# Mixer A of a hybrid layer: the turns of one shared PSUM bank moved to other steps of a selective scan

## What is computed

```python
xn = rmsnorm(layernorm(x)) * norm_w
x_part, z = split(xn @ in_proj_w.T)
u = silu(causal_conv(x_part, conv_w, 4 taps) + conv_b)
dt, B, C = split(u @ x_proj_w.T)              # 8, 16 and 16 columns
delta = softplus(dt @ dt_proj_w.T + dt_proj_b)
h = exp(delta * A) * h + delta * B * u        # for each time step, 256 x 16 states
y = (h * C).sum(states) + u * D
out = (y * silu(z)) @ out_proj_w.T + residual
```

## The kernel before

| use | writer on PE | reader |
|---|---|---|
| TAPS0, TAPS1 | convolution, 4 taps, two at a step (L334) | ACT, bias added, into u (L488) |
| PROJECT (chunk g - 1) | output projection (L364) | DVE `add` (L582), end of step 4 |
| XPROJ | dt, B and C rows (L352) | ACT `keep_rows` (L464, L465), then DVE `low_rows` (L570), end of step 7 |
| DT0, DT1 | dt projection (L358) | ACT `parts` (L468, L469) |
| Z0, Z1 | gate input z (L340) | ACT copy (L516) |

## Time and profile before

### The profile page before, as it was taken

The page is one execution under the profiler, slowest core; times in us unless marked ns, Lnnn a source line. Parts: engine busy times, 40 slices in busy tenths (PEclk is TensorE's granted clock), DMA queues, the critical chain, the costliest instruction groups (busy, mean ns, idle before and its releaser), DMA issues. The chain is left out here.

```text
span 1163.9 us, 16413 instructions
## 1 busy us (share of the span) xinstructions
PE 1014.3 (87%) x4830; PEld 718.0 (62%) x4830; DVE 750.9 (65%) x1167; ACT 609.5 (52%) x1154; POOL 575.7 (49%) x455
## 2 busy tenths in 40 slices
PE   5887879788788889999999787896897899999997
PEld 2222323232246669999998444653575689999996
DVE  4788777779929755555555476755469555555555
ACT  5665453555335345555554486667542455555553
POOL 2368565567710488733851364631000887454732
PEclk9889889789978999999999888997978999999999
DMA  4122111212231113321110400000320223111103
GB/s 134 57 60 67 47 63 46 64 53 71 59 121 55 56 33 93 77 83 60 35 42 15 111 1 1 1 1 0 103 73 3 70 82 91 52 53 59 53 26 113
DMA packets 57248, 66.41 MB, mean 57 GB/s; under 512 B 6088, under 2 KB 40656, under 8 KB 57168
## 3 DMA queue, kind: packets, MB, share of 16 engines
q1 hardware_dynamic: 52176, 55.13, 15.3%
q0 software_dynamic: 4992, 10.23, 3.6%
HBM read 54.86 MB, written 10.49 MB: 56 GB/s over the span
## 5 line engine op out<-in xcount | busy, mean ns | idle before, releaser
L687 POOL TENSOR_TENSOR a_hc<-a_h,a_c_sb 128x512 f32<-128x512 f32 x128 | 160.4, 1267 | 105.1 <-DVE a_h L608 90.2
L533 ACT ACTIVATE ps<-a_delta,a_neg_a 128x512 f32<-128x512 f32 x128 | 87.7, 688 | 125.9 <-DVE a_h L608 125.4
L419 PE MATMUL ps<-a_hc,eye 128*128 128x512 f32 x256 | 141.4, 669 | 12.1 <-POOL a_hc L687 11.9
L419 PEld LDWEIGHTS ps<-a_hc,eye 128*128 128x128 f32 x256 | 49.3, 211 | 85.6 <-issue 50.9
L592 DVE TENSOR_TENSOR a_b_u<-a_du,ps 128x1024 f32<-128x1024 f32 x64 | 76.6, 1196 | 38.5 <-PE ps L406 38.4
L879 POOL CAST g_ring_rounded<-g_ring 128x1876 fp32r<-128x1876 f32 x8 | 14.1, 1761 | 153.1 <-DVE g_table L1394 103.5
L608 DVE TENSOR_TENSOR_SCAN a_h<-ps,a_state,a_b_u 128x512 f32<-128x512 f32 x64 | 78.8, 1262 | 0.0
L1023 PE MATMUL ps<-g_ring_rounded,g_q_hi_rounded 128*128 x312 | 77.0, 337 | 0.0
L1023 PE MATMUL ps<-f_ring_rounded,f_q_hi_rounded 128*128 x312 | 77.0, 337 | 0.0
L608 DVE TENSOR_TENSOR_SCAN a_h<-ps,a_b_u 128x512 f32<-128x512 f32 x64 | 75.1, 1206 | 0.2
L879 POOL CAST f_ring_rounded<-f_ring 128x1876 fp32r<-128x1876 f32 x8 | 14.1, 1759 | 115.0 <-DVE f_table L1394 70.7
(11 more groups left out here) (450 smaller groups left out, 2874.0 us busy)
## 6 DMA issues: line engine op xcount, KB each, us to landing
a_c_sb<-c_rows SPq DMA_DIRECT2D x64, 256.0 KB, 3.2
f_ring<-in_gu SPq DMA_DIRECT2D x16, 469.0 KB, 4.6
g_ring<-in_gu SPq DMA_DIRECT2D x16, 469.0 KB, 4.4
f_ring<-in_dn SPq DMA_DIRECT2D x8, 512.0 KB, 6.2
g_ring<-in_dn SPq DMA_DIRECT2D x8, 512.0 KB, 5.7
xn_rows<-f_work SPq DMA_DIRECT2D x8, 256.0 KB, 2.6
f_rows<-token_rows SPq DMA_DIRECT2D x8, 256.0 KB, 4.9
xn_rows<-g_work SPq DMA_DIRECT2D x8, 256.0 KB, 2.6
```

The costliest lines, as they stand in the source:

```text
L419: nc.tensor.matmul(ps[:, Y + f, :], k.eye[:, :], hc[:, s % WAITING, :], start=False, stop=(n == NST - 1)).then_inc(y_added, 1)
L533: nc.scalar.activation(ps[:, A + m % NA, :], delta[:, f, cols(g)], ACT.Exp, scale=neg_a[:, f, n:n + 1])\
L687: nc.gpsimd.tensor_tensor(hc[:, m % WAITING, :], h[:, s % DEPTH, :], c_sb[:, i % RING, :], ALU.mult)\
```

## The change

Only numbers in four `between` parts change. In step or half-step numbers, with the chunk that is being scanned:

| use | PE step | reader's half-step on ACT |
|---|---|---|
| TAPS0, both tap pairs | 0, 1 (as before) | 4 -> 2 |
| TAPS1, both tap pairs | 2, 3 -> 3, 4 | 8 -> 7 |
| PROJECT | 4 -> 6 | (DVE, end of step 4, as before) |
| XPROJ | 6 -> 8 | 14 -> 15 (DVE, end of step 7, as before) |
| DT0, DT1 | 8, 9 -> 10, 12 | 18, 20 -> 19, 23 |
| softplus exp, log | | 21, 22 -> 24, 25 |
| Z0, Z1 | 11, 12 -> 14, 15 | 25, 27 -> 27, 30 |

On POOL delta goes from half-step 21 to 24, du from 23 to 26, and the addition to x from 27 to 14. The queues of DVE and SP hold the same instructions in the same order. No instruction is added or taken away, and each keeps its waits.

```diff
@@ PE
-                    if n in (0, 2):
-                        in_turn(g, TAPS0 + n // 2)
-                    if n in (1, 3):
-                        convolution(g + 1, n // 2, O, TAPS // 2, TAPS).then_inc(o_ready, 1)
-                if g and n == 4:
+                    if n in (0, 3):
+                        in_turn(g, TAPS0 + n // 3)
+                    if n in (1, 4):
+                        convolution(g + 1, n // 4, O, TAPS // 2, TAPS).then_inc(o_ready, 1)
+                if g and n == 6:
                     in_turn(g, PROJECT)
...
@@ POOL
-                    if s == 27:
+                    if s == 14:
                         pool.wait_ge(norm.normed, g + 1)
```

More of the change, by code:

```diff
@@ L385, in between @@
                 if g + 1 < NCH:
-                    if n in (0, 2):
-                        in_turn(g, TAPS0 + n // 2)
-                    if n in (1, 3):
-                        convolution(g + 1, n // 2, O, TAPS // 2, TAPS).then_inc(o_ready, 1)
-                if g and n == 4:
+                    if n in (0, 3):
[3 more added lines that the diff above has]
+                if g and n == 6:
                     in_turn(g, PROJECT)
                 if g + 1 < NCH:
-                    if n == 6:
+                    if n == 8:
                         in_turn(g, XPROJ)
[L395 to L398, removed]
+                    if n in (10, 12):
+                        in_turn(g, DT0 + (n - 10) // 2)
+                    if n in (14, 15):
+                        in_turn(g, Z0 + n - 14)
             def broadcast(m):
@@ L484, in between @@
                 if c < NCH:
-                    if s in (4, 8):
-                        f = s // 8
+                    if s in (2, 7):
+                        f = s // 7
                         turn(g, TAPS0 + f)
@@ L500, in between @@
                 if c < NCH:
-                    if s == 14:
+                    if s == 15:
                         turn(g, XPROJ)
                         keep_rows(c, O)
-                    if s in (18, 20):
-                        f = (s - 18) // 2
+                    if s in (19, 23):
+                        f = (s - 19) // 4
                         turn(g, DT0 + f)
                         parts(c, f, O).then_inc(o_read, 1)
-                    if s == 21:
+                    if s == 24:
                         softplus_exp(c)
-                    if s == 22:
+                    if s == 25:
                         softplus_log(c)
                         nc.scalar.preload_act_table_set("exp_and_others")
-                    if s in (25, 27):
-                        f = (s - 25) // 2
+                    if s in (27, 30):
+                        f = (s - 27) // 3
                         turn(g, Z0 + f)
@@ L694, in half_sequence @@
                                 .then_inc(delta_ready, 1)
-                        if s == 23:
+                        if s == 26:
                             pool.wait_ge(delta_ready, g + 2)
```

## The result

The changed kernel takes 1121.08 us (median of four runs, 1114.49 to 1122.36) against 1169.82 before (a fourth run, 1170.82, has joined the three of the table); the ratio is 0.958, with a 95% interval of 0.954 to 0.962. The profiled execution, at 1114.49 the fastest of them, has a span of 1112.7 us, 51.2 less than before. The last `add` of mixer A now ends at 281.70 us in place of 328.45, and the scan started at the same time (43.83 and 43.81), so 46.75 of the 51.2 us are gained inside mixer A.

A forecast was written before the change was run, and what follows sets the result against it. DVE was taken to set mixer A's pace, delayed by PE's queue waits. Of 53.8 us of waits 48.8 go and 4.2 come: 44.6 us off 1165.75 gives 1121.1, stated as 1123 us, range 1116 to 1138.

The forecast's parts named there:

- The bound: Mixer A: DVE sets the pace, but waits 53.8 us, nearly all on PE, which is late through waits in its queue.
- What goes: Of DVE's 53.8 us of waits in mixer A, 48.8 can go; the drain's 2.45 and 2.14 stay.
- the gates' share: DVE's waits at the gates of chunks 0 and 1, 10.6 of 13.3 us, are among what goes.
- The load of PE: PE's whole work per chunk of mixer A, put at 54.9 us, should fit within DVE's time.
- In chunk 0 with nothing to spare: PE's 54.9 us against DVE's 54.5 us in chunk 0: fits, without room.
- What comes instead: New DVE waits in five places of mixer A, 3.7 us, with 0.5 for small shifts: 4.2 us.
- ACT's block at half-step 9: DVE waits 0.5 us in chunks 0 and 2, 0.3 in chunk 1; its later start in chunk 0 adds 1.3.
- The gates of chunks 0 and 1: New DVE waits for the last accumulations: 0.3 us at each, 0.5 more in chunk 0, 1.1 us together.
- The log block: ACT's softplus log at half-step 25: 8.8 us of work fits DVE's 9.0, costing 0, at worst 1 us a chunk.
- small shifts: Allowance of 0.5 us for small shifts of mixer A's `add` against PE.
- the signs that were named: Wait limits, last `add` near 283 us, chunks 0 to 2 granted 0.95 or more of the clock.
- The total: Gain of 44.6 us in mixer A: profiled execution 1121.1 us, median forecast 1123 us.
- Rival A: PE's short new waits cost the clock, 2.4 us each in nine places; 11 to 13 us come back; chance 0.12.

The follow-up runs named there:

- e1: Kernel before with only PE's steps moved as in the change; ratio to before 0.970, mixer A's scan time 253.3 us.
- e2: Kernel before with only ACT's and POOL's half-steps moved as in the change; ratio to before 0.9995, scan time 286.6 us.
- e3: Kernel before with only TAPS0, TAPS1, PROJECT and XPROJ moved, on PE and ACT; 1150.03 us.
- e4: Kernel before with only DT, Z, softplus and POOL's delta and du moved; 1129.03 us.
- e9: The changed kernel itself, traced and timed again; median 1120.23 us, ratio to before 0.957.
- e8: Changed kernel with XPROJ, DT1, Z0, Z1 one PE step earlier and ACT and POOL half-steps retuned by a queue search; 1114.56 us.
- e12: The kernel of e8 run again, unaltered; 1113.34 to 1114.42 us in five runs, ratio to before 0.952.
- e11: The kernel of e12 with step 10's broadcast done 5 times more and step 14's 7 times more on PE; median 1110.25 us, ratio to before 0.950.
- e6: Changed kernel with DT0 one PE step earlier, 9 in place of 10; scan time 246.5 us.
- e10: Kernel before with 5, 8, 16 and 14 unread PE products ahead of TAPS1, PROJECT, DT0 and Z1, chunks 0 to 2; ratio to before 0.985.
- e5: Kernel before with 3, 5, 9 and 8 unread PE products ahead of TAPS1, PROJECT, DT0 and Z1, also in chunk 3; ratio to before 0.991.

## Why the prediction was right

**The bound.** "PE's idle time is on the critical path although its load is below DVE's" held: e1 and e2 part the two sides; PE's steps carry 31.3 of the 46.8 us alone, and the other 15.4 come only when the readers move with them.

**What goes.** 48.8 us were to go; the list after shows all of L406's and the gates' share gone, and of the drain, 0.7 went as well: the last gates wait 1.43 and 0.53 us in place of 2.45 and 0.17, and the last `add` 2.14 as before:

```profile
276.96 0.69 DVE L577 TENSOR_TENSOR a_yz<-ps,a_sz 128x512 f32<-128x512 f32 x1 [1.43 <-PE ps L419]
278.19 0.69 DVE L577 TENSOR_TENSOR a_yz<-ps,a_sz 128x512 f32<-128x512 f32 x1 [0.53 <-PE ps L419]
281.01 0.69 DVE L582 TENSOR_TENSOR x<-x,ps 128x512 f32<-128x512 f32 x1 [2.14 <-PE ps L364]
```

Only 0.2 of it can come from the addition to x, which used to stand among POOL's last products: e1, e3 and e4 leave it there, and their last gates wait 1.62 to 1.63 and 0.53 us. The rest is the clock in the one trace of before: its last eight accumulation rows took 5.26 us, with 0.72 granted from 320 to 325 us, and in e3 4.79 at 1.00.

**The load of PE.** "In chunk 0 with nothing to spare" counted an output projection that chunk 0 doesn't have (PROJECT is that of the chunk before). Without it the sum is 53.0 us against DVE's 54.5, and PE was busy 50.4 of 57.0 us there.

**What comes instead.** 4.2 us were summed, 3.4 came. The first was the scan of chunk 0 that waits for ACT's block at half-step 9, forecast at 0.5 + 1.3 us:

```profile
63.22 1.22 DVE L608 TENSOR_TENSOR_SCAN a_h<-ps,a_b_u 128x512 f32<-128x512 f32 x1 [1.16 <-ACT ps L533]
```

It measured 1.16. PE brought TAPS1's second pair about 1.2 us earlier than I had worked out: ACT read it at 55.77 us and not at 57.0. In chunk 1 nothing came of the 0.3, in chunk 2 0.36 for the 0.5. The gates of chunks 0 and 1 waited 0.46 + 0.17 and 0.36 + 0.17, 1.16 against 1.1. The log block, put at 0 with 0.2 to spare, cost 0.19 in chunks 0 and 2. The "small shifts", 0.5, were 0.37 at one `add`. Parts, not only the sum, were about right. Of the signs that were named, one failed: chunk 2 was granted 0.94 and not 0.95 of the clock.

**The total** was right partly by luck. 44.6 us of gain inside mixer A measured 46.75. The profiled execution came out at 1114.5 and not at 1121.1, because the scan gained 2.2 us more than forecast and the stages behind were also 4.4 us faster in it. The median, 1121.1, is 1.9 us from the forecast of 1123, and this stands on the spread between executions too: the second trace's scan time was 3.8 us longer.

**Rival A was the weak step.** I took a wait under 2.2 us as safe for the clock, because one of 2.18 had been so the earlier trace rows. The changed kernel's first trace has half clock in three places, behind waits of 1.17 and 1.04 us at DT0 of chunks 1 and 2 and of 1.92 us at Z1 of chunk 2 (1.89 us in place of 1.12), e9 after 1.17, e8 and e12 after 1.2. With a chance of 0.12 and a price of 11 to 13 us it was put as all or nothing; in fact it came in part in both traces of the changed kernel. It cost DVE next to nothing in the first, about 1 us in chunk 0 of e9, and 3.3 us in chunk 0 of e8 and e12. So in the first trace the forecast held not because the clock did, but because PE's lead covered the price. e11 shows that the 3.3 us can be had back. The price for each hit, 2.4 us of PE time, was near: e6 shows 3.0.

**The two rules weighed.** ACT's table loads again run without a further drain: in e1 a load at 91.70 takes 1.28 us and the next ACTIVATE starts at 92.99, and the ACTIVATE ahead of the load ended at 91.68, so none stands ahead of it either. The time by the Trainium skill's figure ("ScalarE: Activation LUTs", "What ACT_TABLE_LOAD costs"), 1139 us, was not met. What the Trainium skill says in "TensorE: Matmul & The Clock Gate", section "A second HAM failure mode: psum-queue depth-cycling", that frequent small idles between groups of products make the clock swing between its levels, fits the hits after 1.2 us better than I had allowed, though chunk 3 with a gap in each step is still granted 1.00 in the changed kernel.

**What stays open** is how the 46.8 us divide between order and clock. e10 gives 9.9 us as a lower bound, and the rows of before an estimate of 19. A filler that holds the clock through all of the waits of before was not found.

## To carry to other kernels

On an engine with an in-order queue, place each turn of a shared buffer by when its previous reader is done on the pacing engine's clock, and write both positions on that one clock; an engine with spare capacity can still set the pace through a wait in front of what others need. Move the writer's and the readers' positions together: the writers alone gave two thirds, the readers alone nothing. Where TensorE has to wait a microsecond or two with work behind it that others need, repeating a product that is needed anyway can be cheaper than the wait (here by 3.4 us, e11 against e12).

## What the runs showed of the hardware

- TensorE's clock after a wait can't be told from the wait's length between 0.7 and 2.2 us. It stayed full after 1.18 and 1.92 us (changed kernel, DT0 and Z1 of chunk 0), 2.18 (before, TAPS1 of chunk 1) and 2.20 (e4, TAPS1 of chunk 2). It fell to half behind 0.69 (e4, DT0 of chunk 0), 1.04 and 1.17 (changed kernel, DT0 of chunks 2 and 1), 1.18 (e1 and e12) and 1.92 (changed kernel, Z1 of chunk 2). Two executions of one kernel differed at DT0 of chunk 0 after the same wait (1.18 full, 1.17 half).
- The fall can come one product late: in e5 DT0 ran in 1.16 us after a wait of 2.52, and the accumulation behind it took 3.59 us in place of 1.98.
- Work in front of a shortened wait didn't always hold it. In e10 PE ran 3.9 us of broadcast products (0.23 us each), waited 1.27 us, and fell to half 1.0 us after it had begun again; there, at Z1, it was slow after waits of 0.7 to 1.1 us behind the same filler. In e11, where five or seven of these products took the place of the wait and the fp32 ones followed after less than 0.9 us, it stayed at 1.00 in all four chunk windows.
- One chip took about 120 us longer for everything behind mixer A and the same for mixer A. There PE's weight loads in the expert stages show idle time that nothing in the profile releases, 74.9 us in four pieces (weight loads of e1, 300 to 1253 us); the first trace of the changed kernel has no such pieces:

```profile
PEld ps L1023 <- issue: 74.9, 4, 22.3
```
